# A two-layer mixture-of-experts kernel on one core: member transposes moved in among the experts, shared steps moved ahead, and three of eight weight splits given to POOL

## The chip, the cores and the metric

The kernel runs on one core of one Trainium2 chip, as one launch. The metric is the device time of one execution in microseconds (us); lower is better. The engines are TensorE (PE, with its weight loads shown as PEld), VectorE (DVE), ScalarE (ACT), GpSimd (POOL) and SyncE (SP, which issues transfers). They run their own instruction streams and meet only at semaphores.

## The reference, cut to what matters

Two layers run over 1024 tokens of width 256. Each normalises `x`, computes an attention-like branch `s` and a mixture `g`, and sets `x = x + s * silu(mixture)`. Only the first layer's mixture is touched:

```python
scores = sigmoid(x @ router_w.T)            # 32 experts in 8 groups, top 3 groups, top 4 experts
...                                         # each (token, expert) pair gets a slot; C = 40 slots per expert
Xp = x[slots_token].reshape(E, C, d)        # E = 32, d = 256
G = einsum('ecd,edi->eci', Xp, W_gate)      # i = 128
U = einsum('ecd,edi->eci', Xp, W_up)
Y = einsum('eci,eid->ecd', silu(G) * U, W_down)
out = zeros.at[slots_token].add(Y.reshape(EC, d) * slots_w[:, None])
shared = silu(x @ shared_gate.T) * (x @ shared_up.T) @ shared_down.T
return out + shared
```

## The kernel before, in words

Matrices are multiplied as pairs of float16: a high part and a low part (value minus high part), three products for each pair. Splitting an expert's weights means making `w_h` (rounded, times 64) and `w_l` (the rest) from the loaded float32 `wf`, all [128 x 768].

**`route0`** scores the tokens. DVE picks experts (`sel16`, L414), PE counts positions with triangular matrices (L309, L310), and DVE makes the 0/1 matrix `member` (L428): for each of 8 token tiles, 128 tokens by 1280 slots. PE multiplies it into the tokens to gather each expert's inputs (L323, L325), and then into the routing weights (L332, L333). PE also computes the shared experts' gate and up projections in four steps (`shared_gate_up`, L299, two float32 banks of 512 a step): two before the positions and two after them. Each step is followed on ACT by `sg` and `up` (L359, L360) and by the high halves of one expert's weights (L350, L352), and on POOL by the product `shared_hT` (L385) and the low half (L374). The first eight experts' weights are split here.

**`experts0`** runs the 32 experts in four rounds of eight, written by the helper `rounds`: for each step b, each engine does its listed jobs, some of them three steps late. A job for expert b that is three steps late runs at step b+3, so that a round has eight full steps and three short ones (a tail). The next round starts behind the tail on each engine. The jobs, in each engine's order:

- PE: `down(b-3)` (L513 to L515), `gate_up(b)` (L501 to L503).
- ACT: `silu(b)` makes `sg` (L524), `next_high(b-3)` makes the next round's `wh` (L535), `hidden_high(b)` makes `hh` (L529).
- DVE: `hidden(b)` makes `hf` (L542), `next_low(b-3)` makes `wl` (L558), `hidden_low(b)` makes `hl` (L547), `outputs(b-3)` writes `yT` (L552).

The last round makes no weights. `down` needs `hl`; `next_high` needs `down`; `hf` needs `sg`; `hh` needs `hf`; `hl` needs `hh`. `down` uses four PSUM banks in turn. POOL only makes `xT_h` and `xT_l` here (L566, L568).

**`combine0`** brings the experts' outputs back to the tokens. PE turns `member` (L599, ten 128x128 transposes a token tile, through PSUM banks 2 and 3) and ACT copies it to one of two `turned` buffers (L633). PE turns `yT` (L607), DVE scales it into `yw_h`, `yw_l` (L643, L646), and then for each of eight token tiles PE turns the next tile's members and runs 20 products of width 256 (L619, L620) and the shared part (L622). POOL splits the first two heads' weights of the attention that follows (L705, L707, L709).

Of the kernel before, what the change touches and what calls it, by code (L numbers as in the profile page):

```python
# [213 lines left out]
def route0(nc, env, router_w, e_bias):  # L214
# [6 lines left out]
    with ExitStack() as local:  # L221
# [39 lines left out]
        with nc.Block() as block:  # L261
            @block.sync
            def _(sp):

                for e in range(EB):
                    load_expert(sp, env, e, e)
                for b in range(EB):
                    sp.wait_ge(w_ready, b + 1)
                    load_expert(sp, env, EB + b, b)

            @block.tensor
            def _(pe):
# [29 lines left out]

                for step in range(2 * IC - 2):
                    shared_gate_up(step)
# [6 lines left out]
                last.then_inc(pos_ready, 1)  # L311
                for step in range(2 * IC - 2, 2 * IC):
                    shared_gate_up(step)

                pe.wait_ge(up_done, 2 * IC)
# [54 lines left out]
            @block.gpsimd  # L370
            def _(pool):
                def weights_low(e):
                    pool.wait_ge(w_high, 2 * e + 2)
                    pool.tensor_tensor(w_l[e][:, :, :], wf[e][:, :, :], w_h[e][:, :, :], ALU.subtract).then_inc(w_ready, 1)  # L374


                xn = env["xn"]
                pool.tensor_copy(xn_h[:, :, :], xn[:, :, :]).then_inc(high_done, 1)
                pool.wait_ge(high_done, 1)
                pool.tensor_tensor(xn_l[:, :, :], xn[:, :, :], xn_h[:, :, :], ALU.subtract).then_inc(xn_split, 1)  # L380
                for step in range(2 * IC):
                    t, ic = step // IC, step % IC
                    pool.wait_ge(silu_done, step + 1)
                    pool.wait_ge(up_done, step + 1)
                    pool.tensor_tensor(hT[:, ic, t * HALF:(t + 1) * HALF], up[:, step % 2, :], sg[:, step % 2, :],  # L385
                                       ALU.mult).then_inc(h_ready, 1)
                    weights_low(step)
                for e in range(2 * IC, EB):
                    weights_low(e)
# [50 lines left out]

EB = 8


# [11 lines left out]
def experts0(nc, env):  # L455
# [3 lines left out]
    with ExitStack() as local:  # L459
        def tmp(name, shape, dt=F32):  # L460
            return local.enter_context(nc.sbuf_tensor("e0_" + name, shape, dt))
        BANKS = 4
        sg, hf = ([tmp(f"{n}{b}", [P, CAP]) for b in range(BANKS)] for n in ("sg", "hf"))
        h_h, h_l = ([tmp(f"{n}{b}", [P, CAP], F16) for b in range(BANKS)] for n in ("hh", "hl"))
        wh_ready, gu_ready, silu_done, h_ready, hh_ready, hl_ready, y_ready, y_done, x_high = (
            sem("e0_" + s) for s in ("nwh", "gu", "si", "h", "hh", "hl", "y", "yd", "xh"))

        def rounds(engine, *jobs):
# [12 lines left out]
        with nc.Block() as block:  # L481
            @block.sync
            def _(sp):
                with sp.Fori(0, E0 // EB - 2) as i:
                    for b in range(EB):

                        sp.wait_ge(w_ready, EB * i + EB + b + 1)
                        load_expert(sp, env, EB * i + 2 * EB + b, b)

            @block.tensor  # L490
            def _(pe):
                def gate_up(i, b):
                    pe.wait_ge(w_ready, EB * i + b + 1)

# [9 lines left out]
                    last.then_inc(gu_ready, 1)  # L504

                def down(i, b):

                    pe.wait_ge(hl_ready, EB * i + b + 1)
                    hh, hl = h_h[b % BANKS][:, :], h_l[b % BANKS][:, :]
                    for c in range(DC):  # L510
                        out = psum[:, BANKS + b % BANKS, c * CAP:(c + 1) * CAP]
                        wh, wl = w_h[b][:, 2 * DC + c, :], w_l[b][:, 2 * DC + c, :]
# [3 lines left out]
                    last.then_inc(y_ready, 1)  # L516
                rounds(pe, (3, down, False), (0, gate_up, False))

            @block.scalar
            def _(act):  # L520
# [10 lines left out]
                def next_high(i, b):  # L531
# [3 lines left out]
                    act.activation(w_h[b][:, :, :], wf[b][:, :, :], ACT.Copy, scale=WSCALE).then_inc(wh_ready, 1)  # L535
                rounds(act, (0, silu, False), (3, next_high, True), (0, hidden_high, False))

            @block.vector
            def _(dve):
# [10 lines left out]
                def outputs(i, b):  # L550
                    dve.wait_ge(y_ready, EB * i + b + 1)
                    dve.tensor_scalar(yT[:, :, bass.ds((EB * i + b) * CAP, CAP)],  # L552
                                      psum[:, BANKS + b % BANKS, 0:DC * CAP].rearrange("p (c s) -> p c s", c=DC),
                                      1.0 / WSCALE, None, ALU.mult).then_inc(y_done, 1)

                def next_low(i, b):
                    dve.wait_ge(wh_ready, EB * i + b + 1)
                    dve.scalar_tensor_tensor(w_l[b][:, :, :], wf[b][:, :, :], WSCALE, w_h[b][:, :, :],  # L558
                                             ALU.mult, ALU.subtract).then_inc(w_ready, 1)
                rounds(dve, (0, hidden, False), (3, next_low, True), (0, hidden_low, False), (3, outputs, False))  # L560

            @block.gpsimd
            def _(pool):

                high, low = env["xT_h"], env["xT_l"]
                pool.tensor_copy(high[:, :, :], xnT[:, :, :]).then_inc(x_high, 1)  # L566
                pool.wait_ge(x_high, 1)
                pool.tensor_tensor(low[:, :, :], xnT[:, :, :], high[:, :, :], ALU.subtract)  # L568


def combine0(nc, env):

    sem, psum, ident, ident16 = (env[k] for k in ("sem", "psum", "ident", "ident16"))
    member, yT, w_slot, gate0, hT, w3T = (env[k] for k in ("member", "yT", "w_slot", "gate0", "shared_hT", "shared_wT"))
    IC = IS // P
    with ExitStack() as local:
        def tmp(name, shape, dt=F32):
            return local.enter_context(nc.sbuf_tensor("c0_" + name, shape, dt))

        yw_h, yw_l = tmp("yw_h", [P, ST, D], F16), tmp("yw_l", [P, ST, D], F16)  # L580
        turned = [tmp(f"turned{b}", [P, ST, P], F16) for b in range(2)]
        y_ready, yh_done, yl_done, m_ready, m_done, o_ready, o_done = (
            sem("c1_" + s) for s in ("y", "yh", "yl", "m", "md", "o", "od"))
        mcuts = [(0, 8), (8, ST - 8)]
        with nc.Block() as block:
# [4 lines left out]
            def _(pe):  # L590
                def turn_members(n):
                    slots = member[:, n, :, :].rearrange("p e c -> p (e c)")
                    for k, (at, size) in enumerate(mcuts):
                        step = 2 * n + k
                        if step >= 2:
                            pe.wait_ge(m_done, step - 1)
                        for s in range(at, at + size):
                            out = psum[:, 2 + k, :].bitcast(F16)[:, (s - at) * P:(s - at + 1) * P]
                            last = pe.transpose(out, slots[:, s * P:(s + 1) * P], ident16[:, :])  # L599
                        last.then_inc(m_ready, 1)  # L600

                turn_members(0)
                for s in range(ST):
# [5 lines left out]
                for n in range(NT):  # L609
                    if n + 1 < NT:  # L610
                        turn_members(n + 1)
                    pe.wait_ge(m_done, 2 * n + 2)
                    if n == 0:
# [4 lines left out]
                    for s in range(ST):  # L618
                        pe.matmul(out, turned[n % 2][:, s, :], yw_h[:, s, :], start=(s == 0), stop=False)  # L619
                        pe.matmul(out, turned[n % 2][:, s, :], yw_l[:, s, :], start=False, stop=False)  # L620
                    for ic in range(IC):
# [5 lines left out]
            def _(act):  # L627
                for n in range(NT):
                    for k, (at, size) in enumerate(mcuts):
                        act.wait_ge(m_ready, 2 * n + k + 1)  # L630
                        if n >= 2:
                            act.wait_ge(o_ready, n - 1)
                        act.copy(turned[n % 2][:, at:at + size, :].rearrange("p s x -> p (s x)").bitcast(F32),  # L633
                                 psum[:, 2 + k, 0:size * P // 2]).then_inc(m_done, 1)
                for n in range(NT):
# [17 lines left out]
def mixture0(nc, env, w):  # L653

    with ExitStack() as local:
# [12 lines left out]
        with ExitStack() as experts:  # L668
# [5 lines left out]
            env["w_h"], env["w_l"] = ([part(f"w{x}{b}", [P, 3 * DC, P], F16) for b in range(EB)] for x in "hl")  # L674
            env["w_high"], env["w_ready"] = env["sem"]("e0_wh"), env["sem"]("e0_w")
            env["expert_loaded"] = [env["sem"](f"expert_loaded{b}") for b in range(EB)]
            env["expert_weights"] = [w["L0_ffn_" + k] for k in ("W_gate", "W_up", "W_down")]
            route0(nc, env, w["L0_ffn_router_w"], w["L0_ffn_e_bias"])
            experts0(nc, env)
        combine0(nc, env)  # L680
# [2092 lines left out]
```

## Time and profile before

| | us |
|---|---|
| median of 3 runs | 1194.45 (1194.11 to 1199.62) |
| the profiled execution, its own time | 1192.11 |
| its span in the trace | 1190.4 |
| routing, from the first shared step to the last routing product | 26.2 to 73.8 |
| the experts' block | 75.7 to 121.7 |
| `combine0` | 122.1 to 162.5 |
| PE busy over the span | 1045.4 (88%) |
| DVE busy over the span | 842.4 (71%) |
| ACT busy over the span | 628.1 (53%) |
| POOL busy over the span | 586.6 (49%) |

The changed stages are the first 14% of the span. What comes behind them waits for the end of `combine0` at a barrier, and so it moves with that end. In the trace a duration is an instruction's own; the distance to the next start on the same engine is what it costs when the engine is full.

### The profile page before, as it was taken

What the parts mean: (1) busy time and instruction counts of PE and PEld (TensorE: products, weight loads), DVE (VectorE), ACT (ScalarE), POOL (GpSimd) and SP (SyncE); (2) the same over time, 40 slices, a digit from 0 to 9 for tenths busy, and PEclk for the clock granted to TensorE, in tenths of its full rate; (3) what the DMA queues carried; (4) which work ended last, traced back from release to release, by engine and by line L of the source; (5) the groups of instructions that cost most, each with busy time, mean ns of one, the idle gap of its engine ahead of it and who ended that gap; (6) DMA issues with size and microseconds to landing.
All of it is one profiled execution on the core that took longest, in us unless ns stands there. A gap on an engine that the chain in (4) does not pass through costs nothing. (4 is left out here: it accounts for less than half of the span.)

```text
span 1190.4 us, 23472 instructions
## 1 busy us (share of the span) xinstructions
PE 1045.4 (88%) x7870; PEld 697.7 (59%) x7870; DVE 842.4 (71%) x1461; ACT 628.1 (53%) x1241; POOL 586.6 (49%) x449
## 2 busy tenths in 40 slices
PE   6776878999999999789999999999978967878797
PEld 4355666666666666556666666657833335457444
DVE  3958427687878787667778778884579955856557
ACT  3536137666666666556666666662351024645531
POOL 3540325586657665745776575543228302531164
PEclk9875799999999999989999999999999978989899
DMA  5136120976786666538657755565102316658832
GB/s 169 40 102 179 28 53 1 108 79 76 82 103 73 94 64 105 78 48 100 75 92 68 100 77 84 48 87 146 46 30 80 111 62 206 205 187 274 284 92 89
DMA packets 186058, 119.82 MB, mean 101 GB/s; under 512 B 64548, under 2 KB 179286, under 8 KB 185686
## 3 DMA queue, kind: packets, MB, share of 16 engines
q1 hardware_dynamic: 170070, 97.35, 46.2%
q10 hardware_dynamic: 12800, 12.58, 3.0%
q0 software_dynamic: 3072, 8.39, 2.1%
q8 instruction: 66, 1.08, 0.5%
q14 instruction: 50, 0.41, 0.2%
HBM read 81.90 MB, written 36.37 MB: 99 GB/s over the span
## 5 line engine op out<-in xcount | busy, mean ns | idle before, releaser
L1297 DVE TENSOR_REDUCE a_nmax<-psum 128x1 f32<-128x1024 f32 x128 | 156.1, 1219 | 80.0 <-PE psum L1145 76.1
L1303 DVE SCALAR_TENSOR_TENSOR a_pT<-psum,a_pT 128x512 f16<-128x512 f32 x256 | 164.9, 684 | 22.3 <-ACT a_pT L1240 16.7
L1240 ACT ACTIVATE a_pT<-psum 128x512 f16<-128x512 f32 x256 | 140.4, 604 | 18.1 <-PE psum L1156 11.7
L1058 POOL TENSOR_TENSOR a_rnorm<-a_ss,a_power 128x8 f32<-128x8 f32 x32 | 58.3, 1823 | 181.6 <-DVE a_ss L1273 181.6
L1232 ACT ACTIVATE a_ex<-psum,a_nmax 128x1024 f32<-128x1024 f32 x128 | 142.8, 1116 | 9.4 <-issue 8.6
L1156 PEld LDWEIGHTS psum<-ident,a_ex 128*128 128x128 f32 x1024 | 119.5, 141 | 25.8 <-DVE a_pT L1303 1.4
L1156 PE MATMUL psum<-ident,a_ex 128*128 128x128 f32 x1024 | 133.3, 273 | 0.0
L1127 PE MATMUL psum<-a_wh,xT_h 128*128 128x128 f16 (+1 forms) x512 | 115.6, 248 | 2.0 <-PEq L2738 2.0
L1129 PE MATMUL psum<-a_wh,xT_l 128*128 128x128 f16 (+1 forms) x512 | 115.4, 248 | 0.3 <-issue 0.3
L1128 PE MATMUL psum<-a_wl,xT_h 128*128 128x128 f16 (+1 forms) x512 | 115.5, 248 | 0.0
L1167 PE MATMUL psum<-a_pT,a_vh 128*128 128x512 f16 x256 | 97.5, 381 | 14.8 <-DVE a_of L976 13.7
L1169 PE MATMUL psum<-a_pT,a_vl 128*128 128x512 f16 x256 | 97.5, 381 | 0.0
L1168 PE MATMUL psum<-a_pT,a_vh 128*128 128x512 f16 x256 | 97.5, 381 | 0.0
L1209 ACT ACTIVATE sq<-psum 128x512 f32<-128x512 f32 x64 | 38.3, 599 | 102.2 <-PE psum L1129 100.6
L810 POOL TENSOR_TENSOR a_e_wh<-a_e_wf,a_lifts 128x768 f16<-128x768 f32 x47 | 68.9, 1466 | 37.7 <-DMA a_e_wf<-in_L_ffn_swd 16.2
L814 POOL TENSOR_TENSOR a_e_wh<-a_e_wf,a_e_wh 128x768 f16<-128x768 f32 x47 | 81.4, 1731 | 3.7
L1141 PE MATMUL psum<-a_qkTh 128*128 128x512 f16 x256 | 76.2, 379 | 2.5 <-ACT a_ex L1232 1.3
L1145 PE MATMUL psum<-a_qkTh,a_qkTl 128*128 128x512 f16 x256 | 76.1, 379 | 0.0
L1143 PE MATMUL psum<-a_qkTl,a_qkTh 128*128 128x512 f16 x256 | 76.1, 379 | 0.0
L812 POOL TENSOR_TENSOR a_e_wf<-a_e_wf,a_lifts 128x768 f32<-128x768 f32 x47 | 68.9, 1467 | 3.7
L1765 POOL TENSOR_TENSOR g_e_hl<-g_e_hf,g_e_hh 128x128 f16<-128x128 f32 x48 | 25.8, 540 | 91.2 <-DVE g_e_hh L1757 89.8
L1216 ACT ACTIVATE a_qkTh<-psum,a_qk_scale 128x512 f16<-128x512 f32 x64 | 42.3, 686 | 53.5 <-PE psum L1114 53.5
(394 smaller groups left out, 2584.0 us busy)
## 6 DMA issues: line engine op xcount, KB each, us to landing
split_gate_up<-a_e_wh SPq DMA_DIRECT2D x64, 128.0 KB
a_rb<-row_scales SPq DMA_DIRECT2D x32, 256.0 KB, 4.2
g_e_gu<-split_gate_up SPq DMA_DIRECT2D x32, 256.0 KB, 3.8
block_outputs<-g_e_ym ACTq DMA_DIRECT2D x16, 512.0 KB, 4.4
split_rest<-a_e_wh SPq DMA_DIRECT2D x45, 128.0 KB
wf<-in_L_ffn_W_gate SPq DMA_DIRECT2D x32, 128.0 KB, 2.5
wf<-in_L_ffn_W_up SPq DMA_DIRECT2D x32, 128.0 KB, 2.5
wf<-in_L_ffn_W_down SPq DMA_DIRECT2D x32, 128.0 KB, 3.0
```

The lines of the kernel that those rows point to most:

```text
L814: pool.tensor_tensor(low, whole, high, ALU.subtract).then_inc(self.ready, 1)
L1127: pe.matmul(dst, xh, wh, start=(c == 0), stop=False)
L1128: pe.matmul(dst, xh, wl, start=False, stop=False)
L1129: last = pe.matmul(dst, xl, wh, start=False, stop=(c == DC - 1))
L1156: last = pe.transpose(out[:, k * P:(k + 1) * P], ex[m % 2][:, (4 * h + k) * P:(4 * h + k + 1) * P], ident[:, :])
L1167: pe.matmul(out, vh[:, k, :], ph, start=(k == 0), stop=False)
L1168: pe.matmul(out, vh[:, k, :], pl, start=False, stop=False)
L1169: last = pe.matmul(out, vl[:, k, :], ph, start=False, stop=(k == KT - 1))
L1232: act.activation(ex[m % 2][:, :], score_banks(m), ACT.Exp, bias=nmax[:, m % 2:m % 2 + 1], accum_out=total[g][:, k:k + 1]).then_inc(exp_rea ...
L1240: act.activation(pT[g][:, 0, 4 * h:4 * h + 4, (m % 4) * P:(m % 4 + 1) * P], bank_of(r, unit).rearrange("p (k q) -> p k q", k=4), ACT.Copy, ...
L1297: dve.tensor_reduce(nmax[:, k:k + 1], score_banks(m), AX.X, ALU.max, negate=True).then_inc(max_ready, 1)
L1303: dve.scalar_tensor_tensor(low, bank_of(r, unit).rearrange("p (k q) -> p k q", k=4), PROB, high, ALU.mult, ALU.subtract).then_inc(low_done, 1)
```

## The change

It has four parts. First, both later `shared_gate_up` steps run before PE waits for the selected experts. Second, the 80 transposes of `member` go from `combine0` into `experts0`: behind `gate_up(b)` PE turns two or three slot tiles (`turn_members`, PSUM banks 6 and 7), ACT copies them (`members_out`, last job of its step) and all are kept in one array. Third, `down` has two PSUM banks instead of four and waits for the `outputs` of the expert two before it (`y_done` starts at 2). Fourth, the low halves of experts 1, 4 and 7 of each round are made by POOL in two instructions instead of by one of DVE.

```diff
@@ route0, PE
-                for step in range(2 * IC - 2):
+                for step in range(2 * IC):
                     shared_gate_up(step)
                 pe.wait_ge(sel_ready, 1)
...
                 last.then_inc(pos_ready, 1)
-                for step in range(2 * IC - 2, 2 * IC):
-                    shared_gate_up(step)
@@ module
+POOL_LOWS = (1, 4, 7)
+def maker_of(b):
+    return 1 if b in POOL_LOWS else 0
+def lows_made(i, b):
+    mine = [e for e in range(EB) if maker_of(e) == maker_of(b)]
+    return i * len(mine) + mine.index(b) + 1
@@ experts0, SP and PE (each wait on w_ready)
-                        sp.wait_ge(w_ready, EB * i + EB + b + 1)
+                        sp.wait_ge(w_ready[maker_of(b)], lows_made(i + 1, b))
@@ experts0, PE
+        CUTS = [(0, 3), (3, 3), (6, 2), (8, 2)]
+                def turn_members(i, b):
+                    at, size = CUTS[b % 4]
+                    tile = member[:, bass.ds(2 * i + b // 4, 1), :, :].rearrange("p n e c -> p (n e c)")
+                    pe.wait_ge(m_done, EB * i + b + 1)
+                    for s in range(size):
+                        last = pe.transpose(psum[:, 6 + b % 2, :].bitcast(F16)[:, s * P:(s + 1) * P],
+                                            tile[:, (at + s) * P:(at + s + 1) * P], ident16[:, :])
+                    last.then_inc(m_ready, 1)
                 def down(i, b):
                     pe.wait_ge(hl_ready, EB * i + b + 1)
+                    pe.wait_ge(y_done, EB * i + b + 1)
-                        out = psum[:, BANKS + b % BANKS, c * CAP:(c + 1) * CAP]
+                        out = psum[:, BANKS + b % 2, c * CAP:(c + 1) * CAP]
-                rounds(pe, (3, down, False), (0, gate_up, False))
+                rounds(pe, (3, down, False), (0, gate_up, False), (0, turn_members, False))
@@ experts0, ACT
+                def members_out(i, b):
+                    at, size = CUTS[b % 4]
+                    act.wait_ge(m_ready, EB * i + b + 1)
+                    act.copy(turned[:, bass.ds(2 * i + b // 4, 1), at:at + size, :].rearrange("p n s x -> p (n s x)").bitcast(F32),
+                             psum[:, 6 + b % 2, 0:size * P // 2]).then_inc(m_done, 1)
-                rounds(act, (0, silu, False), (3, next_high, True), (0, hidden_high, False))
+                rounds(act, (0, silu, False), (3, next_high, True), (0, hidden_high, False), (0, members_out, False))
@@ experts0, DVE: next_low only where maker_of(b) == 0
@@ experts0, POOL
+                pool.memset(spare[:, 0:1], 0.0).then_inc(m_done, 2)
+                pool.memset(spare[:, 1:2], 0.0).then_inc(y_done, 2)
                 pool.tensor_copy(high[:, :, :], xnT[:, :, :]).then_inc(x_high, 1)
...
+                pool.memset(lift[:, :], WSCALE).then_inc(x_high, 1)
+                def next_low(i, b):
+                    if maker_of(b) == 1:
+                        pool.wait_ge(wh_ready, EB * i + b + 1)
+                        pool.tensor_tensor(whole, whole, lift[:, 0:1].to_broadcast([P, 3 * DC * P]), ALU.mult).then_inc(scaled, 1)
+                        pool.wait_ge(scaled, len(POOL_LOWS) * i + POOL_LOWS.index(b) + 1)
+                        pool.tensor_tensor(low_part, whole, high_part, ALU.subtract).then_inc(w_ready[1], 1)
+                rounds(pool, (3, next_low, True))
@@ combine0: turn_members, its waits and ACT's 16 copies are gone
-                        pe.matmul(out, turned[n % 2][:, s, :], yw_h[:, s, :], start=(s == 0), stop=False)
+                        pe.matmul(out, turned[:, n, s, :], yw_h[:, s, :], start=(s == 0), stop=False)
```

## Rows read from the trace of the kernel before

**Rows 1.** Stretches: length; busy us of PE, PEld, DVE, ACT, POOL; PEclk; DMA; GB/s

```profile
33.30:40.80 7.50, 0.00 (x0) 0.00 (x0) 6.77 (x30) 2.66 (x4) 3.91 (x3) 0.70 0.35 105
...
52.40:69.70 17.30, 17.23 (x96) 9.31 (x97) 9.47 (x6) 9.34 (x15) 14.95 (x7) 1.00 0.42 122
77.00:119.00 42.00, 24.98 (x522) 22.05 (x521) 36.12 (x108) 27.14 (x82) 4.24 (x2) 0.50 0.52 151
```

**Rows 2.** Timeline of the experts: ACT's `hh` of step 2 in rounds 1, 2, 4

```profile
81.52 0.24 ACT L529 ACTIVATE e_hh<-e_hf 128x40 f16<-128x40 f32 x1 [3.62 <-DVE e_hf L542]
...
93.18 0.24 ACT L529 ACTIVATE e_hh<-e_hf 128x40 f16<-128x40 f32 x1 [0.28 <-DVE e_hf L542]
...
116.94 0.24 ACT L529 ACTIVATE e_hh<-e_hf 128x40 f16<-128x40 f32 x1 [0.28 <-DVE e_hf L542]
```

**Rows 3.** Timeline: one full step of round 1 on DVE, then on ACT

```profile
84.98 0.19 DVE L542 SCALAR_TENSOR_TENSOR e_hf<-psum,e_sg 128x40 f32<-128x40 f32 x1
85.08 0.95 DVE L558 SCALAR_TENSOR_TENSOR wl<-wf,wh 128x768 f16<-128x768 f32 x1
85.95 0.20 DVE L547 TENSOR_TENSOR e_hl<-e_hf,e_hh 128x40 f16<-128x40 f32 x1
86.06 0.24 DVE L552 TENSOR_SCALAR yT<-psum 128x80 f32 x1
...
85.20 0.24 ACT L529 ACTIVATE e_hh<-e_hf 128x40 f16<-128x40 f32 x1 [0.17 <-DVE e_hf L542]
85.34 0.19 ACT L524 ACTIVATE e_sg<-psum 128x40 f32<-128x40 f32 x1
85.43 0.83 ACT L535 ACTIVATE wh<-wf 128x768 f16<-128x768 f32 x1
```

**Rows 4.** Timeline: shared steps on PE (two runs of sixteen products), `member` on DVE

```profile
26.16 7.13 PE L299 MATMUL psum<-xnT,shared_wT 128*128 128x512 f32 x16 [0.69 <-ACT shared_wT L344]
...
41.84 9.46 PE L299 MATMUL psum<-xnT,shared_wT 128*128 128x512 f32 x16
...
44.69 16.37 DVE L428 TENSOR_TENSOR member<-r_place,steps 128x1280 f16<-128x1280 f32 x8
```

**Rows 5.** Line L428: count, duration ns min/median/max, starts

```profile
L428 DVE TENSOR_TENSOR member<-r_place,steps x8: 1485/2024/2937, 44.7 to 58.1; 128x1280 f16<-128x1280 f32 x8
```

**Rows 6.** Timeline: pairs of POOL and DVE instructions that overlap in time

```profile
77.26 4.06 POOL L568 TENSOR_TENSOR xT_l<-xnT,xT_h 128x2048 f16<-128x2048 f32 x1
...
77.79 3.58 DVE L547 TENSOR_TENSOR e_hl<-e_hf,e_hh 128x40 f16<-128x40 f32 x1 [0.30 <-ACT e_hh L529]
...
252.05 1.47 POOL L812 TENSOR_TENSOR a_e_wf<-a_e_wf,a_lifts 128x768 f32<-128x768 f32 x1
...
252.89 1.17 DVE L981 TENSOR_TENSOR oT_l<-a_of,oT_h 128x512 f16<-128x512 f32 x1
...
253.59 1.98 POOL L814 TENSOR_TENSOR a_e_wh<-a_e_wf,a_e_wh 128x768 f16<-128x768 f32 x1
```

**Rows 7.** Timeline: POOL's scaling and subtraction of one head's weights; an undisturbed L981

```profile
127.13 1.47 POOL L707 TENSOR_TENSOR a_wf<-a_wf,a_lifts 128x768 f32<-128x768 f32 x1
128.68 1.64 POOL L709 TENSOR_TENSOR a_wl<-a_wf,a_wh 128x768 f16<-128x768 f32 x1
...
237.00 0.68 DVE L981 TENSOR_TENSOR oT_l<-a_of,oT_h 128x512 f16<-128x512 f32 x1
```

**Rows 8.** `combine0`: member transposes on PE at both clocks; ACT's copies (ns)

```profile
131.71 1.27 PE L599 MATMUL psum<-ident,member 128*128 128x128 f16 x10
133.15 0.37 PE L619 MATMUL psum<-c_yw_h,c_turned 128*128 128x256 f16 x1 [0.16 <-DVE c_yw_l L646]
...
137.24 0.72 PE L599 MATMUL psum<-ident,member 128*128 128x128 f16 x10
137.79 0.27 PE L619 MATMUL psum<-c_yw_h,c_turned 128*128 128x256 f16 x1
...
L633 ACT COPY c_turned<-psum x16: 271/429/586, 123.2 to 156.4; 128x512 f32<-128x512 f32 x8, 128x128 f32<-128x128 f32 x8
```

More of the change, by code:

```diff
@@ L267, in _ @@
                 for b in range(EB):
-                    sp.wait_ge(w_ready, b + 1)
+                    sp.wait_ge(w_ready[maker_of(b)], lows_made(0, b))
                     load_expert(sp, env, EB + b, b)
@@ L462, in experts0 @@
         BANKS = 4
+        member, ident16, turned = env["member"], env["ident16"], env["turned"]
+        CUTS = [(0, 3), (3, 3), (6, 2), (8, 2)]
+        m_ready, m_done = sem("e0_m"), sem("e0_md")
         sg, hf = ([tmp(f"{n}{b}", [P, CAP]) for b in range(BANKS)] for n in ("sg", "hf"))
@@ L492, in gate_up @@
                 def gate_up(i, b):
[L493 removed]
+                    pe.wait_ge(w_ready[maker_of(b)], lows_made(i, b))
                     slots = bass.ds((EB * i + b) * CAP, CAP)
@@ L552, in outputs @@
                     dve.tensor_scalar(yT[:, :, bass.ds((EB * i + b) * CAP, CAP)],
-                                      psum[:, BANKS + b % BANKS, 0:DC * CAP].rearrange("p (c s) -> p c s", c=DC),
+                                      psum[:, BANKS + b % 2, 0:DC * CAP].rearrange("p (c s) -> p c s", c=DC),
                                       1.0 / WSCALE, None, ALU.mult).then_inc(y_done, 1)
                 def next_low(i, b):
-                    dve.wait_ge(wh_ready, EB * i + b + 1)
-                    dve.scalar_tensor_tensor(w_l[b][:, :, :], wf[b][:, :, :], WSCALE, w_h[b][:, :, :],
-                                             ALU.mult, ALU.subtract).then_inc(w_ready, 1)
+                    if maker_of(b) == 0:
+                        dve.wait_ge(wh_ready, EB * i + b + 1)
+                        dve.scalar_tensor_tensor(w_l[b][:, :, :], wf[b][:, :, :], WSCALE, w_h[b][:, :, :],
+                                                 ALU.mult, ALU.subtract).then_inc(w_ready[0], 1)
                 rounds(dve, (0, hidden, False), (3, next_low, True), (0, hidden_low, False), (3, outputs, False))
@@ L568, in _ @@
                 pool.tensor_tensor(low[:, :, :], xnT[:, :, :], high[:, :, :], ALU.subtract)
+                pool.memset(lift[:, :], WSCALE).then_inc(x_high, 1)
+                pool.wait_ge(x_high, 2)
+                def next_low(i, b):
+                    if maker_of(b) == 1:
+                        whole, high_part, low_part = (x[b][:, :, :].rearrange("p c i -> p (c i)") for x in (wf, w_h, w_l))
+                        pool.wait_ge(wh_ready, EB * i + b + 1)
+                        pool.tensor_tensor(whole, whole, lift[:, 0:1].to_broadcast([P, 3 * DC * P]), ALU.mult)\
+                            .then_inc(scaled, 1)
+                        pool.wait_ge(scaled, len(POOL_LOWS) * i + POOL_LOWS.index(b) + 1)
+                        pool.tensor_tensor(low_part, whole, high_part, ALU.subtract).then_inc(w_ready[1], 1)
+                rounds(pool, (3, next_low, True))
 def combine0(nc, env):
-    sem, psum, ident, ident16 = (env[k] for k in ("sem", "psum", "ident", "ident16"))
-    member, yT, w_slot, gate0, hT, w3T = (env[k] for k in ("member", "yT", "w_slot", "gate0", "shared_hT", "shared_wT"))
+    sem, psum, ident = (env[k] for k in ("sem", "psum", "ident"))
+    yT, w_slot, gate0, hT, w3T = (env[k] for k in ("yT", "w_slot", "gate0", "shared_hT", "shared_wT"))
     IC = IS // P
@@ L580, in combine0 @@
         yw_h, yw_l = tmp("yw_h", [P, ST, D], F16), tmp("yw_l", [P, ST, D], F16)
[L581 to L584, printed above, removed]
+        turned = env["turned"]
+        y_ready, yh_done, yl_done, o_ready, o_done = (sem("c1_" + s) for s in ("y", "yh", "yl", "o", "od"))
         with nc.Block() as block:
@@ L590, in _ @@
             def _(pe):
[L591 to L602, printed above, removed]
                 for s in range(ST):
@@ L618, in _ @@
                     for s in range(ST):
-                        pe.matmul(out, turned[n % 2][:, s, :], yw_h[:, s, :], start=(s == 0), stop=False)
-                        pe.matmul(out, turned[n % 2][:, s, :], yw_l[:, s, :], start=False, stop=False)
+                        pe.matmul(out, turned[:, n, s, :], yw_h[:, s, :], start=(s == 0), stop=False)
+                        pe.matmul(out, turned[:, n, s, :], yw_l[:, s, :], start=False, stop=False)
                     for ic in range(IC):
@@ L627, in _ @@
             def _(act):
[L628 to L634, printed above, removed]
                 for n in range(NT):
@@ L674, in mixture0 @@
             env["w_h"], env["w_l"] = ([part(f"w{x}{b}", [P, 3 * DC, P], F16) for b in range(EB)] for x in "hl")
-            env["w_high"], env["w_ready"] = env["sem"]("e0_wh"), env["sem"]("e0_w")
+            env["w_high"], env["w_ready"] = env["sem"]("e0_wh"), [env["sem"](f"e0_w{maker}") for maker in range(2)]
             env["expert_loaded"] = [env["sem"](f"expert_loaded{b}") for b in range(EB)]
@@ L678, in mixture0 @@
             route0(nc, env, w["L0_ffn_router_w"], w["L0_ffn_e_bias"])
+            env["turned"] = nc.alloc_sbuf_tensor_at("c0_turned", [P, NT, ST, P], F16, offset=186 * 1024)
             experts0(nc, env)
```

6 lines of the change are left out of this document (2 added, 4 removed).

## Prediction

> **What bounds the kernel now.** I read the stretches first, then the timeline of each changed stage, engine by engine, then every POOL instruction that overlaps a DVE one. Three stages change, and each has its own limit.
>
> In the routing, PE does the last two shared steps only behind the positions: 41.84 to 51.3 [rows 4]. Before that it had done nothing for 7.5 us, in which its granted clock fell [rows 1]. `member` is made from 44.69 to 61.06 on DVE [rows 4], but PE starts to gather only at 52.4. It is then busy for 17.23 of 17.30 us at full clock [rows 1], 2.16 us a token tile. PE sets the end here.
>
> In the experts' block PE is busy for 25.0 of 42.0 us, at granted clock 0.50, the 1.2 GHz level [rows 1]. A full step has a loop through ACT and DVE. On DVE the next instruction starts 0.10 us behind `hf`, 0.87 behind `wl`, 0.11 behind `hl` and 0.15 behind `yT`: 1.23 in all. On ACT it is 0.14 behind `hh`, 0.09 behind `sg` and about 0.8 behind `wh`: 1.03 [rows 3]. DVE sets the pace. From round 1 to round 4 the same `hh` moves from 81.52 to 116.94, so a round takes 11.8 us [rows 2].
>
> In `combine0`, DVE sets the end up to 133.15, and PE from there, at 0.55 us for the ten transposes between two token tiles [rows 8].
>
> **Shared steps moved ahead.** A step takes 7.13 / 2 = 3.5 us at full clock [rows 4]. Steps 2 and 3 fill 33.3 to 40.3, the former idle stretch [rows 1], and end before the selection, which DVE still delivers at 40.8. So the positions and the start of `member` stay where they are. If the cover were gone, the positions would come up to 1 us late. ACT and POOL get the two steps' work earlier. I add it up: the low halves of experts 4 to 7 reach POOL from 44.6 on, when `member` starts. `member` [rows 5] takes 1.49 us alone and up to 2.94 next to POOL: eight at 1.45 to the next start and four low halves at 2.94 - 1.49 = 1.45 end it at 44.7 + 11.6 + 5.8 = 62.1, against 61.1 now. The first tile comes at 46.2 or, behind one low half, at 47.6. PE has then done nothing for some 5 us. The same kind of gap cost the run of 16 products 9.46 - 7.13 = 2.3 us [rows 4]; the gather may pay 0 to 3. Its end: 47.6 + 8 x 2.16 = 64.9, plus 2.3 = 67.2, against 69.7. **-2.5 us**, bounds -4.8 and -1.
>
> **Transposes leave `combine0`.** Ten at half clock (1.27 as a run, some 1.0 to the next start) stand in front of the `yT` chain. The second ten lie under DVE's `yw` work (the wait of 0.16 behind them is for `yw_l`): worth nothing. Six more, at 0.55 each, lie between token tiles on a full PE [rows 8]. -1.0 - 6 x 0.55 = **-4.3 us**, bounds -5.3 and -3, if the clock rises earlier or later. ACT's 16 copies were hidden behind PE.
>
> **Transposes enter the experts.** Two or three an expert at about 0.11 each at half clock [rows 8] make 0.2 to 0.3 us more on PE, which is 60% busy: hidden in the first three rounds. ACT's copies have 128 or 192 float32 columns; the rows are 271 ns for 128 and 586 for 512 [rows 8], so 271 or 323 ns, and 0.17 or 0.22 to the next start if, as for `hh`, 0.1 overlaps. Bounds 0.17 and 0.32. ACT's step grows to 1.23, DVE's own.
>
> **A round without any interference.** I set `hh` of step 2 at 0 and go on by the distances above, 0.03 us from engine to engine. `hh` follows at 1.17, 2.62, 3.84, 5.29 and 6.52 (step 7). `wh(5)` runs 6.84 to 7.67, `wl(5)` to 8.65, `yT(5)` to 8.80. Now `down(7)` waits for that `yT(5)`, where it had a free bank before; `wh(7)` starts at 9.27, and `gate_up(0)` of the next round, queued on PE behind `down(7)`, lets `hh(0)` start at 10.47. Two more head steps of 0.8, 0.2 of it the copy, give `hh(2)` at 12.1. So even with three low halves gone from DVE a round takes 12.1 us, not 11.8: ACT, the copies and the bank wait take back what DVE gains. The last round has no weights; its five steps of 0.73 become about 0.87, PE's `down`, `gate_up` and transposes: **+0.7 us**.
>
> **POOL's low halves.** Each is a scaling of 1.47 us and a subtraction of 1.64, 3.2 us together [rows 7], for a `wl` of 0.95 [rows 3]. They are not free for DVE. `hl` reads `hf` and `hh` from SBUF. It takes 0.20 alone, and took 3.58 when it was issued at 77.79 during a POOL instruction: that one ended at 81.32, `hl` at 81.37. At 252.89 `oT_l`, again with two SBUF inputs, took 1.17 instead of 0.68 [rows 7]; POOL's scaling, the very form used here, ended at 253.52, and the subtraction behind it took 1.98 instead of 1.64 [rows 6]. So a DVE instruction with two SBUF inputs waits for the end of POOL's running one, and POOL's next for it. `hl` and `wl` have two; `hf` and `yT` read one of theirs from PSUM.
>
> The round again with this. POOL's instructions run at 2.49 to 3.96 and 4.04 to 5.68 (expert 1), 8.20 to 9.67 and 9.75 to 11.39 (expert 4), 13.73 to 15.20 and 15.28 to 16.92 (expert 7). Each catches one DVE instruction: `hl(4)`, asked at 2.89, ends at 4.01 (1.1 late); `wl(2)` ends at 6.49 (1.4); `hl(7)` at 9.72 (1.1); `wl(5)` at 12.2 (1.5), and `yT(5)`, `down(7)` and `wh(7)` (12.8 to 13.65) behind it; `hl(0)` of the next round at 15.25 (1.0); `hl(1)` at 16.97 (1.4). That is 7.5 us of blocking. In DVE's queue `yT` and the next `hf` stand behind each, ACT's `hh` waits for that `hf`, and PE for `hl`. Some 2.5 us of it falls into DVE's own waits. `hh(2)` comes at 17.1: 5.2 us more than 11.8. Rounds 1 to 3: 3 x 5.2 = **+15.6 us**. Bounds: +0.9 (3 x 0.3, nothing blocked) and +23 (3 x (12.1 + 7.5 - 11.8), nothing absorbed); I stay at the walk, since both overlaps show a full block.
>
> The Trainium skill (SBUF — State Buffer, "Who interferes with whom") says the port pair that VectorE and GpSimd share is an exclusive lock: whoever issues first has it for the whole instruction, and the other fully blocks, where VectorE has two SBUF inputs and GpSimd reads SBUF. By that rule the round is the walk's; if the two merely shared the rate, the six instructions would at most double, which is the second rival. The trace agrees with the lock: 3.58 us for 0.20 is no sharing.
>
> SP waits for the low halves in the experts' order, so the loads behind 1, 4 and 7 are issued some 3 us later, but each is used a round later: hidden. POOL's added memsets (0.1 each) stand before `xT_h`, ahead of any use.
>
> **The sum.** -2.5 - 4.3 + 15.6 + 0.7 = +9.5 us. The profiled execution took 1192.11 us around a span of 1190.4; with the sum it is 1201.6. It lies 2.3 under the median of 1194.45, so the median goes to **1204.0 us**.
>
> **Rivals.**
> 1. The blocks do bite as walked (forecast): +9.5, 1198 to 1210. Chance 0.67.
> 2. The blocks are partly missed or shared: four `hl` grow by 0.2 and two `wl` by 0.95, 2.7 a round, so a round takes up to 14.8. -6.1 + 3 x 3.0 = +2.9: 1197.4. For it: starts shift by tenths from round to round, and some instruction may slip through between scaling and subtraction. Against it: 3.58 for 0.20. Chance 0.16.
> 3. The other side: POOL's work lies beside DVE's without a block, 12.1 a round. -6.1 + 0.9 = -5.2: 1189.3, and 1187 if the gather pays no clock. It decides if a round stays under 11.8 + 6.1 / 3 = 13.8 us, that is, if the blocks add less than 1.7 to the 12.1. For it: POOL's 9.6 us fit a round, and DVE loses 3 x 0.87. Against it: both overlaps. Chance 0.17.
> 4. The routing gains nothing, since `member`, now ending 1.0 later, bounds the gather: it would end at 62.1 + 2.2 = 64.3, before PE's own 67.2, so DVE is not the bound. Chance 0.0 as a case of its own. What it could cost is inside the bound of -1.
>
> **From these the chances.** 0.5% is 6 us, about what a measurement of this kernel can tell from no change. Case 1 lies above +6 in 0.57 and within in 0.10; case 2 within; case 3 within in 0.06 and faster in 0.11. Faster 0.11, same 0.32, slower 0.57. The range is 1188 to 1210: it takes in most of case 3 and stops where about one in ten of case 1's upper bound is left. Case 1 alone: 1198 to 1210.
>
> **What would show it.** In the trace after: `hl` and `wl` rows in the experts of 1 us and more that end 0.05 us behind a POOL instruction (at three rounds, some 18), with a mean of `hl` near 0.6 and not 0.3; `hh` of step 2 about 17 us apart; PE idle in front of `down` behind them. The routing's gather ending 2 to 3 us earlier, its first tiles at half clock. `combine0` some 4 us shorter, with no transposes of `member`. The forecast is wrong if `hh` of step 2 stays 12 to 13 us apart, or if `down` waits more for `yT` than I give it.

## The result, and the profile after

The changed kernel takes 1216.91 us (median of 4 runs, 1215.97 to 1223.34) against 1194.28 for the kernel before: ratio 1.0195, interval 1.0158 to 1.0231, so **+22.6 us**. Forecast were +9.5 and at most +15.5: the direction is right, the size is not. A second comparison (e6 below) gave +21.4.

The stages of both profiled executions, in us:

| | before | after |
|---|---|---|
| last product of the shared steps starts | 50.7 | 41.8 |
| first `member` tile starts | 44.7 | 48.8 |
| `hh` of step 2, round 1 | 81.5 | 82.2 |
| the same, round 4 | 116.9 | 135.9 |
| last `hh` | 120.6 | 140.7 |
| last `yT` | 121.5 | 142.0 |
| last copy of `combine0` on DVE | 162.1 | 179.3 |
| end of the span | 1190.4 | 1214.8 |

The rounds are 17.9 us long and not 11.8 [rows 2]; this is ACT's `hh` of step 2 in the four rounds:

```profile
82.22 0.24 ACT L553 ACTIVATE e_hh<-e_hf 128x40 f16<-128x40 f32 x1 [2.68 <-DVE e_hf L571]
...
100.09 0.24 ACT L553 ACTIVATE e_hh<-e_hf 128x40 f16<-128x40 f32 x1 [0.86 <-DVE e_hf L571]
...
117.99 0.24 ACT L553 ACTIVATE e_hh<-e_hf 128x40 f16<-128x40 f32 x1 [0.92 <-DVE e_hf L571]
...
135.85 0.24 ACT L553 ACTIVATE e_hh<-e_hf 128x40 f16<-128x40 f32 x1 [1.17 <-DVE e_hf L571]
```

In round 1 POOL's pairs stand against DVE like this (timeline of POOL, then of DVE):

```profile
84.65 1.47 POOL L608 TENSOR_TENSOR wf<-wf,e_lift 128x768 f32<-128x768 f32 x1 [2.59 <-ACT wh L559]
86.20 1.64 POOL L611 TENSOR_TENSOR wl<-wf,wh 128x768 f16<-128x768 f32 x1
...
85.12 1.06 DVE L576 TENSOR_TENSOR e_hl<-e_hf,e_hh 128x40 f16<-128x40 f32 x1 [0.30 <-ACT e_hh L553]
86.10 0.23 DVE L581 TENSOR_SCALAR yT<-psum 128x80 f32 x1
86.25 0.18 DVE L571 SCALAR_TENSOR_TENSOR e_hf<-psum,e_sg 128x40 f32<-128x40 f32 x1
86.85 1.80 DVE L588 SCALAR_TENSOR_TENSOR wl<-wf,wh 128x768 f16<-128x768 f32 x1 [0.42 <-ACT wh L559]
```

`hl`, 0.20 us alone [rows 3], ends 0.06 behind POOL's scaling; `hf` and `yT`, which read PSUM, pass at 0.18 and 0.23 beside POOL. In the three rounds from 82 to 136 us 12 `hl` and 6 `wl` are over 0.1 us late; they lose 11.2 and 6.9 us. The walk had 12 and 6 too, and 22.5 us.

But a second wait is there that the walk had in the tail alone. The waits of the three rounds (engine and what it was to write, whom it waited for: total, times, longest):

```profile
PE psum L537 <- DVE yT L581: 21.8, 15, 2.3
PEld psum L537 <- DVE e_hl L576: 20.5, 15, 2.4
...
ACT wh L559 <- PE psum L539: 8.7, 6, 1.6
```

`down` waits for `yT` fifteen times, five times a round. And in the routing DVE's small instructions in front of `member` stand beside POOL's earlier work. Timelines of DVE and POOL:

```profile
38.44 1.87 DVE L412 TENSOR_TENSOR r_w<-r_prob,r_sel 128x256 f32<-128x256 f32 x1
40.34 0.42 DVE L413 TENSOR_REDUCE r_wsum<-r_w 128x8 f32<-128x256 f32 x1
...
41.79 1.89 DVE L416 SCALAR_TENSOR_TENSOR r_w<-r_w,r_winv 128x256 f32<-128x256 f32 x1
...
45.23 1.75 DVE L422 CAST wk_h<-r_w 128x256 f16<-128x256 f32 x1
47.01 1.75 DVE L423 TENSOR_TENSOR wk_l<-r_w,wk_h 128x256 f16<-128x256 f32 x1
48.79 2.81 DVE L425 TENSOR_TENSOR member<-r_place,steps 128x1280 f16<-128x1280 f32 x1
...
38.31 1.71 POOL L371 TENSOR_TENSOR wl<-wf,wh 128x768 f16<-128x768 f32 x1 [0.27 <-ACT wf L349]
...
41.75 1.64 POOL L371 TENSOR_TENSOR wl<-wf,wh 128x768 f16<-128x768 f32 x1 [0.26 <-ACT wf L349]
...
45.18 5.07 POOL L371 TENSOR_TENSOR wl<-wf,wh 128x768 f16<-128x768 f32 x3 [0.27 <-ACT wf L349]
```

### The profile page after: what moved, and what is told of

Same layout as the page of the kernel before. It is cut to its first block and busy times, and to the rows that moved or that the text cites. A ratio compares the mean times of both kernels' runs of the same rounds, so it can differ in the third digit from the quotient of the medians.

```text
span 1214.8 us, 23648 instructions
## 1 busy us (share of the span) xinstructions
PE 1056.7 (87%) x7870; PEld 699.8 (58%) x7870; DVE 849.6 (70%) x1452; ACT 630.5 (52%) x1257; POOL 608.3 (50%) x470
## 5 line engine op out<-in xcount | busy, mean ns | idle before, releaser
L1237 ACT ACTIVATE a_qkTh<-psum,a_qk_scale 128x512 f16<-128x512 f32 x64 | 42.2, 685 | 52.4 <-PE psum L1135 52.4
```

## The experiments

Each is named by what is in it. "Front" is the start of the last copy of `combine0` against 162.1 (the kernel before, profiled again, had 162.1 again); "rest" is the measured difference less the front, so the loss or gain behind `combine0`. "us" is the difference of the medians in the first row and, in all others, the ratio less one, of some 1189 us. A front comes from one profiled execution, the "us" from several. With the old order of the shared steps the profiles show two patterns of the routing (last section): in e2, e5, e8, e12 and e14 the gather starts at 47.4 to 50.3 us, in the kernel before and e4, e7, e9, e15 and e16 at 52.0 to 52.5. So the fronts of the first five hold a gain of 2.2 to 3.4 us, by the start or the end of their experts, that no edit of theirs made.

| | ratio (interval) | us | round | front | rest |
|---|---|---|---|---|---|
| changed | 1.0195 (1.0158-1.0231) | +22.6 | 17.9 | +17.2 | 5.4 |
| e6 changed, again | 1.0180 (1.0144-1.0216) | +21.4 | 17.9 | +17.4 | 4.0 |
| e1 changed, lows on DVE | 1.0122 (1.0091-1.0153) | +14.5 | 14.6 | +9.2 | 5.3 |
| e2 POOL lows alone | 1.0108 (1.0086-1.0129) | +12.8 | 16.2 | +10.1 | 2.7 |
| e3 shared steps alone | 1.0023 (1.0006-1.0040) | +2.7 | 11.8 | +0.3 | 2.4 |
| e4 transposes, two banks | 1.0084 (1.0061-1.0106) | +10.0 | 14.6 | +5.4 | 4.6 |
| e5 all undone | 0.9993 (0.9971-1.0016) | -0.8 | 11.8 | -2.1 | 1.3 |
| e7 two banks alone | 1.0080 (1.0044-1.0116) | +9.5 | 14.1 | +8.9 | 0.6 |
| e8 `hl` from PSUM | 1.0013 (0.9983-1.0043) | +1.5 | 14.1 | +0.1 | 1.4 |
| e9 transposes, three banks | 1.0056 (1.0030-1.0082) | +6.7 | 13.8 | +2.7 | 4.0 |
| e10 shared, lows late | 0.9972 (0.9944-1.0000) | -3.3 | 11.8 | -3.1 | -0.2 |
| e11 e9 and e10 | 1.0055 (1.0030-1.0080) | +6.5 | 13.8 | +1.4 | 5.1 |
| e12 one POOL low | 1.0029 (1.0003-1.0055) | +3.4 | 13.8 | +3.0 | 0.4 |
| e13 more PE code | 0.9976 (0.9948-1.0004) | -2.9 | 11.8 | -5.1 | 2.2 |
| e14 kept array | 1.0003 (0.9978-1.0028) | +0.4 | 11.8 | -3.2 | 3.6 |
| e15 before, again | 1.0000 (0.9977-1.0023) | 0.0 | 11.8 | 0.0 | 0.0 |
| e16 transposes, again | 1.0094 (1.0060-1.0127) | +11.2 | 14.5 | +6.0 | 5.2 |

**Apart, and undone.** e1 is the changed kernel without POOL's low halves, e2 to e4 are the kernel before with one part each, e5 has every part undone in the changed file, e6 is the changed kernel again.

```diff
e1: -POOL_LOWS = (1, 4, 7)
    +POOL_LOWS = ()
e2: transposes, banks and shared steps as before; POOL_LOWS = (1, 4, 7)
e3: only the two shared_gate_up steps in front of pe.wait_ge(sel_ready, 1)
e4: only turn_members and members_out in experts0 with the kept array, down in two banks
```

> The changed kernel with all eight low halves of a round on DVE again; everything else stays changed. Theory A (POOL's scaling and subtraction block DVE instructions with two SBUF inputs): the rounds, hh of step 2 to hh of step 2, fall from 17.9 us to about 12.7 to 13.3, no hl is longer than 0.3 us but the one behind xT_l, and the time falls by 14 to 15 us to about 1202 or a little less. Theory B (down's wait for yT with two banks is the bulk; 23 us of PE's waits in the changed kernel name it): the rounds stay above 16 us and the time above 1210.

> The kernel before with only the POOL part of the change: low halves of experts 1, 4 and 7 of a round on POOL; four banks for down, no transposes among the experts, shared steps where they were. Theory A: rounds of 15 to 17 us instead of 11.8, so 10 to 15 us slower than before. Theory B: with no bank wait, DVE gains 3 x 0.87 a round and the rounds fall to about 10.5: 3 to 4 us faster than before.

> The kernel before with only the two shared steps moved in front of the positions. Theory A, carried to the routing (POOL's products and low halves of the moved steps now run beside DVE's placing instructions, which have two SBUF inputs or run SBUF to SBUF, and block them): member starts about 4 us later than before, near 48.8 us, the gather ends where it did, and the time is within 2 us of before. As predicted at first (placing not delayed): the gather ends 2 to 3 us earlier and so does the program.

> The kernel before with only the transposes of member moved among the experts, with ACT's copies and two banks for down. From the prediction: rounds near 13 us instead of 11.8 (+3 to +4 in three), the last round +0.7 to +1.7, combine0 3 to 4 us shorter: 0 to +3 us in all. If the bank wait is the bulk of the loss, the rounds are 15 us and more, and the time is 7 us and more above before.

> The changed kernel with all of its parts undone: order of the shared steps, place of the transposes, four banks, all low halves on DVE. What is left of the change is a second semaphore for the weights and one small memset on POOL. If the stages alone hold the loss, it takes the time of before within 2 us. If something that all the variants share (code, memory placement) costs time behind the changed stages, it is 3 to 5 us slower than before.

> The changed kernel again, beside the others on the same chip, for a second reading of the part behind combine0. The rounds come at 17.9 us again and combine0 ends 17 us later than before; if the 5 us that the first profile showed behind it belong to the change, they come again, otherwise the whole is 17 to 20 us.

Each part alone makes the kernel slower, by 12.8, 10.0 and 2.7 us; the interval of the last only just leaves out no change. (The profiled execution of e3 is the fastest of its twelve, and its first shared step starts 1.3 us earlier than in the kernel before, so its front of +0.3 may be too low by as much.) In the rounds POOL's low halves add 4.4 us and the transposes with two banks 2.8; together they add 6.1, since a wait can hide a wait. e5 is back at the kernel before, within its interval of -0.3% to +0.2%, so nothing else in the file costs more than that.

**The wait for the bank.** e7 takes from the change only the two banks and their wait:

```diff
+                    pe.wait_ge(y_done, EB * i + b + 1)
-                        out = psum[:, BANKS + b % BANKS, c * CAP:(c + 1) * CAP]
+                        out = psum[:, BANKS + b % 2, c * CAP:(c + 1) * CAP]
```

> The kernel before with two banks for down and its wait for the yT of the expert two before; no transposes among the experts, all low halves on DVE. Theory B1 (this wait alone holds PE back: gate_up is queued behind down, so PE no longer runs ahead of DVE, and sg comes late): most of the 2.75 us a round that the transposes' part cost, rounds of 13.5 to 14.5. Theory B2 (the transposes and copies themselves cost it): rounds of 12 to 12.5.

2.3 of e4's 2.8 us a round are this wait, without a single transpose or copy. Two steps of e7, on DVE, PE and ACT (timelines):

```profile
100.87 0.24 DVE L568 TENSOR_SCALAR yT<-psum 128x80 f32 x1
...
103.28 0.96 DVE L575 SCALAR_TENSOR_TENSOR wl<-wf,wh 128x768 f16<-128x768 f32 x1 [0.53 <-ACT wh L551]
104.15 0.19 DVE L563 TENSOR_TENSOR e_hl<-e_hf,e_hh 128x40 f16<-128x40 f32 x1
104.26 0.23 DVE L568 TENSOR_SCALAR yT<-psum 128x80 f32 x1
...
101.25 0.19 PE L529 MATMUL psum<-e_hh,wh 128*128 128x40 f16 x1 [1.17 <-DVE yT L568]
...
102.31 0.20 ACT L540 ACTIVATE e_sg<-psum 128x40 f32<-128x40 f32 x1 [0.83 <-PE psum L518]
102.41 0.83 ACT L551 ACTIVATE wh<-wf 128x768 f16<-128x768 f32 x1
```

It is a loop over two steps: `yT(b-2)` 100.87, `down(b)` 101.25, `gate_up` behind it in PE's queue, `sg` 102.31, `wh(b)` 102.41, `wl(b)` 103.28, `yT(b)` 104.26. That is 3.39 us for two steps, and DVE's own two are 2 x 1.23 = 2.46. With four banks PE ran far enough ahead for the loop not to close.

e9 gives `down` three banks (round number modulo 3) and leaves one for the turned blocks:

```diff
-                    pe.wait_ge(y_done, EB * i + b + 1)
+                    pe.wait_ge(y_done, EB * i + b + (1 if b < 2 else 0))
-                        out = psum[:, BANKS + b % 2, c * CAP:(c + 1) * CAP]
+                        out = psum[:, BANKS + b % 3, c * CAP:(c + 1) * CAP]
-                        psum[:, 6 + b % 2, ...
+                        psum[:, 7, ...
```

> Kernel before with the transposes moved among the experts, but the down products over three banks (by round number modulo 3) and the turned blocks in a fourth. If it is the bank wait that makes the rounds of e4_turns 14.6 us instead of 11.8 (down(b) held for yT(b-2), and gate_up queued behind it), down(b) now waits only for yT(b-3) and rounds go back to 12.0 to 13.0 us, the copies being short (0.3 us each): time within 3 us of before or up to 5 us under it, since the placing's own transposes are gone. Rival, that the turns themselves and their copies on ACT and PE cost the round: rounds stay near 14.5 us and the time near +8 to +10 us.

Neither came: 13.8 us. The wait for `yT` falls from 13.6 us (12 times) in e4 to 3.9 (6), but a new one stands beside it, the turning waits for ACT to empty its single bank:

```profile
PE psum L527 <- ACT c_turned L565: 9.5, 12, 2.2
```

Four of the eight banks are for `gate_up`; in both divisions of the other four that were tried one of the two waits is there. How much of the 2.0 us a round that are left is the wait and how much the turns and copies themselves isn't shown. Not tried: a layout that puts two of them into one bank.

**POOL against DVE.** e8 is e2 with `hl` made from PSUM and `hh`; it leaves out the factor `sg`, so its results are not the layer's and only its time counts; e12 is e2 with one POOL low half a round.

```diff
e8: dve.tensor_tensor(h_l, hf, h_h, subtract) -> dve.scalar_tensor_tensor(h_l, psum, 1/WSCALE, h_h, mult, subtract)
e12: POOL_LOWS = (4,)
```

> The kernel before with three low halves a round on POOL, as in the run with that part alone, but hl is made from PSUM and hh instead of from hf and hh: it leaves out the factor sg in the low half of the hidden values, and has one SBUF input. Theory A (a block only where DVE has two SBUF inputs): hl is never longer than 0.3 us in the rounds, only wl is blocked, and the rounds fall from 16.2 us to 12 to 14. If POOL costs DVE time whatever the inputs, or if POOL's late low halves are what is waited for, they stay at 16.

> Kernel before with the low half of one expert in eight (number 4) on POOL instead of three. If each low half on POOL blocks DVE by its own amount, a round is 11.8 + (16.2 - 11.8)/3 = 13.3 us and the time is a third of e2_pool_lows's: +4 us. Rival: one low half fits beside DVE's slack, rounds stay 11.8 to 12.2 and the time is that of before within 1 us.

The group of `hl` from 76 to 142 us, mean ns of one, first in e2 and then in e8:

```profile
L562 DVE TENSOR_TENSOR e_hl<-e_hf,e_hh 128x40 f16<-128x40 f32 x31 | 16.3, 527 | 6.7 <-ACT e_hh L544 6.7
```

```profile
L562 DVE SCALAR_TENSOR_TENSOR e_hl<-psum,e_hh 128x40 f16<-128x40 f32 x29 | 5.7, 196 | 6.0 <-ACT e_hh L544 6.0
```

With one SBUF input `hl` is never late; `wl` still is, and the kernel wins back 11 of 12.8 us. The 14.1 us in the table is a mean: the first round of e8 takes 15.6 us, since POOL's `xT_l` now holds up a `wl` of it and not an `hl` before it, and the other two take 13.4 each, where those of e2 take 16.3. In e12 one pair of POOL's catches two DVE instructions:

```profile
99.14 1.47 POOL L592 TENSOR_TENSOR wf<-wf,e_lift 128x768 f32<-128x768 f32 x1 [10.65 <-ACT wh L550]
99.51 1.15 DVE L562 TENSOR_TENSOR e_hl<-e_hf,e_hh 128x40 f16<-128x40 f32 x1 [0.30 <-ACT e_hh L544]
100.68 1.65 POOL L595 TENSOR_TENSOR wl<-wf,wh 128x768 f16<-128x768 f32 x1
100.73 2.41 DVE L574 SCALAR_TENSOR_TENSOR wl<-wf,wh 128x768 f16<-128x768 f32 x1
```

It spares DVE 0.87 us and costs it 0.95 + 1.46; the round grows by 2.0 us, near half of what three pairs do.

**The routing.** e10 is e3 with POOL's low halves of experts 2 to 7 held until the last `member` tile; e11 adds e9's turns.

```diff
+                pool.wait_ge(member_ready, NT)
                 for e in range(2, EB):
                     weights_low(e)
```

> Kernel before with the shared steps ahead of the placing, but POOL's low halves of the first experts held until the last member tile is made. If the +3 to +4 us on the start of the member tiles in e3_shared (47.9 us instead of 44.7) came from POOL's low halves beside DVE's small placing instructions, these now take 0.2 to 0.5 us each instead of 1.7 to 1.9 and the first member tile starts at 42 to 45 us, the gather ends 2 to 6 us earlier than in e3_shared, and the time is 2 to 5 us under e3_shared, if the low halves that now come late don't hold the first rounds. Rival: the first member tile is bound by the selection and not by the blocked instructions, then it starts near 47 us still.

> Shared steps ahead with the low halves held back, transposes among the experts with three banks for down, and all low halves of the experts on DVE. If the two theories (bank wait in the rounds, blocked small instructions in the placing) are all that is wrong with the parts, the parts give what they were meant to: rounds of 12 to 13 us, combine0 3 to 4 us shorter, the placing 2 us earlier: 2 to 8 us under before. Rival: turns cost the round by themselves, then +3 to +8 us.

In e10 POOL's first low halves and products are still beside `r_sel`, the first `r_w` (1.87 us) and `r_wsum`. From 41.67 on only the `r_w` beside the last `shared_hT` is late (0.90 us); the others run at their own length, all eight `member` tiles too. But the first that needs the positions now waits 1.17 us for PE:

```profile
38.34 1.87 DVE L414 TENSOR_TENSOR r_w<-r_prob,r_sel 128x256 f32<-128x256 f32 x1
...
41.67 0.43 DVE L418 SCALAR_TENSOR_TENSOR r_w<-r_w,r_winv 128x256 f32<-128x256 f32 x1
43.27 0.42 DVE L421 SCALAR_TENSOR_TENSOR r_keep<-psum,r_sel 128x256 f32<-128x256 f32 x1 [1.17 <-PE psum L310]
...
45.12 0.29 DVE L424 CAST wk_h<-r_w 128x256 f16<-128x256 f32 x1
...
L427 DVE TENSOR_TENSOR member<-r_place,steps x8: 1484/1485/1491, 45.9 to 55.7; 128x1280 f16<-128x1280 f32 x8
```

The first tile starts at 45.9, not at 42 to 45 as hoped: the four shared steps fill PE up to 42.3, and the positions come behind them. `hh` of step 2 comes 3.3 us earlier than before, and the kernel takes 3.3 us less: the fastest version made from these parts, its interval just touching no change. That the routing made the 3.3 us isn't shown, since e14, with the routing of before, has 3.2 in its front too. e11, with e9's turns, takes 6.5 us more than before, and e9 alone 6.7: there the routing gives next to nothing.

**Behind `combine0`.** e13 is e10 with 37 idle-time transposes that shift PE's later code; e14 is the kernel before, with its transposes in `combine0`, but copied into the change's kept array.

```diff
e13: +                for k in range(37):
     +                    pe.transpose(psum[:, 0, 0:P // 2].bitcast(F16), ident16, ident16)
e14: -        turned = [tmp(f"turned{b}", [P, ST, P], F16) for b in range(2)]
     +        turned = env["turned"]        # [P, NT, ST, P], as in the change
```

> Kernel e10_shared_low_late with 37 more transposes of the identity on PE, put where PE is idle in front of the gather (into a bank that the gather overwrites). They compute nothing that is used; what they change is that all later instructions of PE stand further on in its stream, about as far as the moved transposes put them. Theory 1, the 4 to 5 us that the kernels with moved transposes lose behind combine0 come from where PE's later code lies: the time goes 4 to 5 us over e10_shared_low_late (ratio near 1.001), all of it behind combine0. Theory 2, it is the kept array: no change behind combine0, at most 1 us in front of it.

> Kernel before with its transposes where they are, in combine0, but copied into the changed kernel's kept array of all eight token tiles (and its fixed place) instead of into two buffers in turn. Up to the end of combine0 nothing should move by more than 1 us. Theory 1, code position: the time is that of before within 1.5 us, and so is the stretch behind combine0. Theory 2, the kept array's place, or what moves in memory with it: 4 to 5 us over before, all behind combine0.

> Kernel before, unchanged, to have its profile from the same chip as the others of this call: ratio 1.00, and the stretch from the last copy of combine0 to the end of the span within 2 us of 1025, so that the stretches of the others have a base of their own. If it is near 1030 there, the 4 to 5 us lost behind combine0 are chance and no theory is needed.

> Kernel e4_turns again, beside e13 to e15: transposes moved, nothing else. From the medians of its first call some 4 us of its +10 us lay behind combine0. If they are real: +8 to +11 us again, the last copy of combine0 some 5 us later than in e15_before_again and the rest behind it. If they were chance: +5 to +6 us.

The eight comparisons of kernels with the kept array have a rest of 3.6 to 5.4 us, the other nine of -0.2 to 2.7. e14, which has the array and nothing else, is with the first: it gained 3.2 us in front and had only +0.4 in all. e13's 2.2 is with the others. Each rest is uncertain by some 3 us, so it is the grouping that speaks and not one row. And it is only an association: read inside each profiled execution, the stretch from the last copy of `combine0` to the end is 1022.7 to 1035.5 us in the eight with the array and 1016.7 to 1028.7 in the ten others, which overlap, and e14's 1028.8 is that of e13 (1028.7), which has no array; e15 has 1024.6. Which access would get slower was not found.

e13 shows something else. Its 37 transposes run while PE has nothing to do, from 43.6 us on, and the gather behind them starts at full clock, where e10's starts at half (stretch 47.5 to 50 us, first e10, then e13; after the length the busy us of PE, PEld, DVE, ACT and POOL, then the granted clock):

```profile
47.50:50.00 2.50, 2.45 (x7) 1.02 (x8) 2.50 (x2) 2.47 (x4) 0.00 (x0) 0.50 0.00 0
```

```profile
47.50:50.00 2.50, 2.31 (x13) 1.30 (x14) 2.50 (x3) 2.46 (x4) 0.00 (x0) 1.00 0.00 0
```

Its last gather product starts at 64.9 and not at 66.4 us, and its front is 2.0 us better, more than the 1 us expected at most; the whole time doesn't show it (-2.9 for -3.3).

## Why the prediction was wrong

**Routing, forecast -2.5 us, measured +0.7** (+2.7 for e3 as a whole). The failed step is "the positions and the start of `member` stay where they are": the first tile came 4.1 us later. The selection came 2.3 us earlier (the pattern of that execution, not the change: e1, with the same routing, has it at 41.4, behind the 40.5 of before), and DVE's chain behind it lost it, and more, to POOL: six instructions at 0.6 to 1.9 us in place of 0.2 to 0.4, 6.4 us more. I had counted POOL's moved work against `member` alone and not against the small instructions in front of it. The positions didn't stay either: the four shared steps, reckoned to end at 40.3, ended at 42.4, and the positions started at 42.2 for 40.9. e10 parts the two: with POOL's later low halves out of the way `member` still starts 1.2 us late, behind PE, and the other 2.9 us are gone.

**A round without interference, forecast 12.1 us, measured 14.6 (e1).** The failed step is that the bank wait holds `down(7)` only. I followed `yT(5)` to `down(7)` and did not ask, for each full step, how far PE runs ahead. e7 puts 2.3 us a round on this wait alone. With the turns the round misses by 2.5, so 3 x 2.5 = 7.5 us, the largest miss. The prediction's own sign of being wrong, `down` waiting more for `yT` than given, was there: fifteen times for three.

**The blocks: mechanism right, the rounds' sum near only by luck.** They were to bring 12.1 to 17.1, so +5.0. They brought 14.6 to 17.9 in the changed kernel, +3.3, and 11.8 to 16.2 in e2, +4.4: where PE already waits for `yT`, part of a block is hidden. Count and mean were as said (18 late instructions for 18, `hl` 0.66 us for 0.6), but together they lost 18.1 us and not 22.5. The rounds came to +18.2 for +15.6: 7.5 us too little for the bank wait, and 5.1 too much for the blocks. The rule of the Trainium skill (SBUF — State Buffer, "Who interferes with whom"), an exclusive lock where VectorE has two SBUF inputs, holds in e2 against e8. The same section lists casts and single-input scalings among the instructions that can take the shared ports, and reductions as never contending; I had not applied it to the routing, where `wk_h` (a cast) took 1.75 us and the reduction 0.42 beside POOL.

**Last round, forecast +0.7, measured +1.2:** from step 2 to the last `hh` 4.83 us against 3.66. e7, without turns, has 4.67, so that too is the bank wait. From there to the last `yT` came 0.4 more.

**`combine0`, forecast -4.3, measured -3.3** (37.3 us from the last `yT` to the last copy, against 40.6): within its bounds. e4 has -3.8.

**Behind it, forecast nothing, measured 4.0 to 5.4.** Nowhere in the working: I had let everything behind the barrier move with it. It goes together with the kept array in the table; that the array causes it isn't shown, and the cause stays open.

The sum again: +0.7 + 18.2 + 1.2 + 0.4 - 3.3 = +17.2, and 5.4 behind it: +22.6. Rival 2's and rival 3's rounds (14.8 and 12.1) did not occur with POOL's low halves in place, and rival 4's case, `member` bounding the gather, came true in part: PE was idle in front of the gather and then ran its first products at half clock, as this stretch of the changed kernel shows (busy us of PE first, PEclk 0.50):

```profile
48.00:54.00 6.00, 2.25 (x7) 1.02 (x8) 5.97 (x3) 3.47 (x5) 6.00 (x4) 0.50 0.67 191
```

## What to carry to other kernels

A buffer taken from a ring isn't free because the ring's owner is 60% busy: walk the loop that the shorter ring closes, over as many steps as it has buffers, and compare it with the pace. Before work is given to POOL, or comes earlier there, list every DVE instruction that will then run beside it, the small ones in front of the critical start above all. And test parts alone: here each of the three was slower by itself. And before the end of a stage in one profile is put down to an edit, look at the stages that the edit doesn't touch: here the same routing code came in two patterns, some 3 us apart.

## What the runs showed that I had not expected

- DVE's selection in the kernel before is itself late by POOL. In e14 the second shared step ran later (16 products in 9.00 us, not 7.13 [rows 4], at a granted clock of 1.00 in both), so POOL's work missed DVE's `r_es`, which took 1.20 and 0.29 us where it took 2.16 and 1.57 before; the gather started at 47.4 and not at 52.5. As the rows stand, slower products made the routing some 3 us faster. Why they were slower isn't shown. Kernels whose routing code doesn't differ fall into one or the other of these patterns (front -3.2 in e14, 0.0 in e15), so no front is known better than by some 3 us.
- In the last stage of the changed kernel ACT waits up to 3.03 us for a product, though PE's records show products without a gap up to 1166.9:

```profile
1162.52 0.60 ACT L2652 ACTIVATE g_m_sg<-psum 128x512 f32<-128x512 f32 x1 [1.39 <-PE psum L2628]
...
1167.53 0.60 ACT L2652 ACTIVATE g_m_sg<-psum 128x512 f32<-128x512 f32 x1 [3.03 <-PE psum L2628]
```

 The stage (`g_m_hf`, first start to last) takes 35.3 and 35.4 us in the two profiles of the changed kernel, and 32.1 and 34.0 in the two of the kernel before, the second of which has waits of 1.40 and 1.59 there and the first 0.6. e1 and e4, with the kept array, take 32.1 too, and e16, the same kernel as e4, 34.9. So at most part of it belongs to the change, and the array alone doesn't bring it; what stops it stays open.
